# A rolled loop in the first stage of a three-block decoder layer: 24 of 35 hand-unrolled steps become three turns of an eight-step loop

## The reference

```python
x = layernorm(x + attn(x))          # self-attention, 16 heads of 32, relative positions in scores
x = layernorm(x + xattn(x, ctx))    # cross-attention, 16 heads of 64, causal mask
x = layernorm(x + ffn(x))           # slots gather from x, 16 experts, slots give back to x
# inside attn, for each batch b and head h:
scores = (q @ k.T + rel_q + rel_k) / sqrt(32)   # rel_q[l, r] = q[l] . dist_emb[l - r + 511]
probs  = softmax(scores)                        # rel_k[l, r] = k[r] . dist_emb[l - r + 511]
ctx    = probs @ v
```

## Time and profile before

| what | value |
|---|---|
| time of the kernel, median of 3 runs | 3928.76 us |
| lowest and highest | 3926.76 and 3929.56 us |
| the profiled execution, its own time | 3928.76 us |
| its span in the profile | 3927.0 us |
| mean granted TensorE clock | 0.964 |
| instructions | 63130 |
| PE, DVE, ACT, POOL busy | 92%, 55%, 45%, 46% of the span |

### The profile page before, as it was taken

One profiled execution on the slowest core, in us unless ns is written; L12 is line 12 of the kernel. 1 busy time (PEld: TensorE's weight loads), 2 busy tenths in 40 slices (PEclk: granted clock), 3 DMA queues, 4 the chain that ended last, 5 costly groups with the idle time before them and its releaser, 6 DMA issues. The chain is left out here.

```text
span 3927.0 us, 63130 instructions
## 1 busy us (share of the span) xinstructions
PE 3613.9 (92%) x19712; PEld 2256.8 (57%) x19712; DVE 2161.4 (55%) x5872; ACT 1767.8 (45%) x3799; POOL 1822.0 (46%) x1652
## 2 busy tenths in 40 slices
PE   6999999999999999998879999999899978888686
PEld 4777777777777777776445555555455431121253
DVE  4666666666666666666676666666333321111355
ACT  4666666666666666665355555555112100000033
POOL 3666666666666666666217777777211000000112
PEclk8999999999999999999989999999999988989898
DMA  7999999999999999999872222222544259999632
GB/s 273 387 386 383 386 393 386 380 383 388 382 383 393 388 386 382 389 379 349 243 241 96 84 82 84 85 85 71 189 159 143 75 198 417 416 418 415 225 108 107
DMA packets 429679, 1091.54 MB, mean 278 GB/s; under 512 B 25152, under 2 KB 107584, under 8 KB 380224
## 3 DMA queue, kind: packets, MB, share of 16 engines
q1 hardware_dynamic: 412208, 1040.34, 70.8%
q10 hardware_dynamic: 16656, 47.19, 3.1%
q0 software_dynamic: 512, 0.26, 0.0%
HBM read 650.97 MB, written 436.73 MB: 277 GB/s over the span
## 5 line engine op out<-in xcount | busy, mean ns | idle before, releaser
L548 POOL TENSOR_SCALAR a_sc<-a_sc,a_inv 128x512 f32<-128x512 f32 x512 | 822.9, 1607 | 559.3 <-DVE a_inv L491 514.0
L500 DVE COPY a_pt<-a_ps_t 128x512 f32<-128x512 f32 x512 | 353.3, 690 | 527.4 <-PE a_ps_t L232 520.7
L1091 POOL TENSOR_SCALAR b_sc<-b_sc,b_inv 128x128 f32<-128x128 f32 (+3 forms) x512 | 546.2, 1083 | 180.0 <-DVE b_inv L1060 176.7
L370 ACT ACTIVATE a_stage_q<-a_ps_b 128x640 f32<-128x640 f32 x512 | 360.5, 704 | 563.4 <-PE a_ps_b L250 540.2
L1021 ACT ACTIVATE b_sc<-b_sc,b_mx 128x128 f32<-128x128 f32 (+3 forms) x512 | 282.0, 552 | 318.6 <-DVE b_mx L1054 318.3
L360 ACT ACTIVATE a_sc<-a_sc,a_mx 128x512 f32<-128x512 f32 x512 | 369.9, 723 | 59.2 <-DVE a_mx L484 54.5
L484 DVE CUSTOM_DVE_ANT_0 a_sc<-a_ps_s,a_rq 128x512 f32<-128x512 f32 x512 | 353.0, 689 | 67.4 <-PE a_ps_s L222 55.3
L370 ACT ACTIVATE a_stage_k<-a_ps_b 128x640 f32<-128x640 f32 x512 | 357.7, 699 | 0.0
L232 PEld LDWEIGHTS a_ps_t<-a_ident,a_sc 128*128 128x128 f32 x2048 | 247.0, 141 | 145.9 <-issue 140.2
L1054 DVE CUSTOM_DVE_ANT_0 b_sc<-b_ps_s,b_mask 128x128 f32<-128x128 f32 (+3 forms) x512 | 229.4, 489 | 164.4 <-PE b_ps_s L969 160.6
L232 PE MATMUL a_ps_t<-a_ident,a_sc 128*128 128x128 f32 x2048 | 309.1, 274 | 9.3 <-DVE a_pt L500 9.2
(11 more groups left out here) (207 smaller groups left out, 6339.1 us busy)
## 6 DMA issues: line engine op xcount, KB each, us to landing
band_q<-a_stage_q SPq DMA_DIRECT2D x128, 1280.0 KB, 7.0
band_k<-a_stage_k SPq DMA_DIRECT2D x128, 1280.0 KB, 10.0
a_rk<-band_k SPq DMA_DIRECT2D x128, 1024.0 KB, 12.9
a_rq<-band_q SPq DMA_DIRECT2D x256, 512.0 KB, 13.4
d_w<-in_e_W SPq DMA_DIRECT2D x24, 4096.0 KB, 42.9
d_wg<-in_e_Wg SPq DMA_DIRECT2D x16, 4096.0 KB, 28.4
keep<-in_e_W SPq DMA_DIRECT2D x8, 4096.0 KB, 36.3
a_okv<-in_b_wkv ACTq DMA_DIRECT2D x62, 512.0 KB, 8.2
```

What stands on the lines that cost most here:

```text
L370: act.activation(st[h % 2][:, t, :], src, ACT.Copy).then_inc(sem[f"a_{kind}_staged"], 1)
L500: dve.tensor_copy(pt[:, h % 2, :, t * P:(t + 1) * P], ps_t[:, :].rearrange("p (r n) -> p r n", r=T4)).then_inc(sem["a_pt_out"], 1)
L548: pool.tensor_scalar(sc[n][:, :], sc[n][:, :], inv[:, n:n + 1], None, ALU.mult)\
L1091: pool.tensor_scalar(sc[j % 2][i][:, 0:width(i)], sc[j % 2][i][:, 0:width(i)], inv[j % 2][:, i:i + 1], None, ALU.mult).then_inc(sem["b_nor ...
```

## The change

`steps` of the self-attention stage writes out quads -2, -1 and 0, then runs quads 1 to 24 as three turns of a machine loop whose body is eight quads, then writes out quads 25 to 32. The same 35 steps run in the same order with the same buffers. `steps` is called once for each of the five engines, so each gets its own loop.

```diff
         def steps(e, quad):
 
-            for g in range(-2, QUADS + 1):
+            for g in (-2, -1, 0):
+                quad(g, g % 4)
+            with e.Fori(1, QUADS - 7, 8) as g:
+                for j in range(8):
+                    quad(g + j, (1 + j) % 4)
+            for g in range(QUADS - 7, QUADS + 1):
                 quad(g, g % 4)
```

## The result

The changed kernel took 3958.14 us (median; 3953.12 to 3960.28) against 3927.76 us before, a ratio of 1.0072 with a 95% interval of 1.0057 to 1.0086: slower by 0.7%, 30 us, three times the forecast 9.6 us and outside the range. The profiled execution took 3950.47 us, at the low end of what the executions showed.

The account below looks back on a forecast made before the run. The prediction took PE, busy 98.8%, to bound self-attention. Two edges at 2.6 (branch delay) + 1.7 (clock) + 0.5 (fetch) = 4.8 us gave 9.6 us on 3928.76, so 3938.4 us, range 3932 to 3949.

Parts of the forecast that it names:

- What bounds the stage: Self-attention: PE sets the pace, busy 98.8% of four quads, so each microsecond its stream stands still is lost.
- where the branch comes: PE's branch ahead of quad 9 at about 573.1, sequencer 1.5 us ahead; delay 2.6 us there and at quad 17.
- The fetch beside heavy traffic: At both self-attention edges, fetching the branch target beside DMA share 1.01 adds 0.5 us per edge; bounds 0 and 5.5.
- The clock: Behind PE's stall at both self-attention edges the clock falls to the lower level, costing 1.7 us each.
- The other engines: DVE, ACT, POOL and SP stall at the same edges under cover: cost 0; without cover up to 3.1 us per edge.
- Register operations: Counts and addresses from registers inside the loop cost 0; upper bound 5 us where the product with v waits for DVE.
- The rival of the slow fetch: At self-attention's edges the branch stands twice as long, 7.4 us; two edges cost 19.4 us, time 3948.2; chance 0.12.

Follow-up runs that it names:

- the run without taken branches: Changed kernel with three loops of one turn each (quads 1 to 8, 9 to 16, 17 to 24) replacing one loop of three turns; 3934.93 us against 3926.02.
- aligned heads: Changed kernel with each engine's loop body placed at the start of a fetch block; 3947.56 us, ratio 1.0057.
- six turns: Changed kernel with the same 24 quads as six turns of a four-quad body, five taken branches instead of two; 3992.48 us against 3923.65.

## Why the prediction was wrong

**What bounds the stage** and **where the branch comes** were right: PE's branch at 573.1 with 1.5 us of queued matmuls as its only cover, at both edges.

**The fetch beside heavy traffic** is the step that failed: "I stay near the lower end: 0.5 us per edge". It was 4.0 and 3.5 us (7.73 and 7.24 us against 3.71). I argued from how long a packet of code takes once it moves, 1.2 us. That is not the wait until it starts. In straight-line code such a wait need not show, since nothing stands still as long as the next packet is there in time; that is my account of why no row showed it. In the trace the first packet of PE's code starts 5.3 us after the changed kernel's branch, in cross-attention 1.1 us. The upper bound from the same rows, 5.5 us, was near. With this term alone right, the sum would have been 2 x 4.3 + 4.0 + 3.5 = 16.1 us, so 3944.9: it is the largest single error and a third of the missing time.

**The clock** was right in kind and too small: I took 1.7 us per edge, and what is left of the edges beside their idle times is 4.1 and 2.8 us, behind idle times of 6 us and a second one of about 3.

**The second idle time** was in no term and no rival. It is 2.54 and 3.06 us, and the place of the loop's head in its block of code, which no row of the profile before shows, decides it.

**The other engines** at no cost was right for this kernel (the loop on PE alone loses as much), but the price "if the cover is gone", 6 us, was less than half of what it is: without PE's loop the two edges cost 6.1 and 7.0 us of the 15.3.

**Register operations** I took as 0, with the place where they would show and 5 us as the bound. The place was right for most quads; the price is 3.3 us between quads 1 and 25 in the run without taken branches. In the changed kernel the quads away from the edges lost 5.7 us, 2.8 of them in the two quads in which PE also waits for ScalarE, a place that I had not named. Why cross-attention had shown 0 is not tested.

**The rival of the slow fetch** was the right one, with a chance of 0.12. Its 19.4 us fell 11.0 short of the 30.4 measured, by the second idle time and its clock and by the quads between the edges: 9.7 per edge against 12.4 makes 5.4, and those quads 5.7 us. That its branch of 7.4 us met the measured 7.73 and 7.24 is partly luck, since doubling was a guess and no row gave the factor.

Open are two things: how the wait for a fetch follows from what is queued ahead of it, and why POOL stands for 5 us at its branch in heavy and in light traffic.

## What to carry to other kernels

A taken branch to code that the engine no longer holds costs a fetch, and the same branch cost 3.8 or 7.7 us here by the stage's DMA traffic: price it from a stall under the same traffic, or give it the upper bound. The time that loads beside it take from issue to landing told the two apart, and the DMA share did not. Before a loop is rolled up, look at how far each sequencer is ahead of its engine at the edge, since that is all the cover there is, and count the edges, not the loops. Look also at the loops behind it: in the trace of the one-turn loops a later loop's branch cost 3.7 us more. If a loop must be, a prefetch hint takes the stall off the edges and leaves one of about half of one edge's price at the exit (6 to 7 us against 12 here), so it should pay the more, the more branches are taken.

## What the runs showed of the hardware that I had not expected

- PE's branch back in self-attention stood for 7.1 to 7.8 us in the stage's full traffic (eleven branches in four kernels: the changed one, PE alone, aligned heads, six turns), and for 3.8 us with a quarter to a half of the band bytes. In all of them it ended 1.3 to 1.7 us after the packet of code had.
- SyncE's branch with a four-quad body cost 0.3 us, all five times, and with the eight-quad body 6.6 and 6.2 us, which fits a short body that is still at hand. PE's four-quad body, about 1480 matmuls and as many weight loads, was not.
- The hinted exits cost 6.2 and 6.7 us, where the exit of the changed kernel's loop cost nothing to be seen: quad 25 was as long as before within 0.5 us.
- The Trainium skill, "Runtime: NRT & Kernel Launch", section "Instruction fetch mechanics", gives a forced fetch of the target as a reason for full unrolling; the 12.1 us per edge of the run with six turns agree with it. With the hint the edges of the eight-quad loop cost under 1 us, and what remains of that reason is the exit.
